# The last gathered slot on its own, the second block buffer cleared by DMA, and new instruction orders in a one-core recommendation tower

## The reference

```python
e = jnp.stack([tbl_0[ids[:, 0]], ..., tbl_49[ids[:, 49]]], axis=1)   # (512, 50, 16)
gram = jnp.einsum('bid,bjd->bij', e, e)
z = gram[:, _I_IDX, _J_IDX]                                          # the pairs i < j
h = jnp.concatenate([z, dense_ctx], axis=1)
h = jnp.maximum(h @ W_top1 + b_top1, 0.0)                            # 512
h = jnp.maximum(h @ W_top2 + b_top2, 0.0)                            # 256
y = h @ W_top3                                                       # 1
```

## Time and profile before

| | before |
|---|---|
| median of 3 runs | 134.31 us (133.75 to 134.50) |
| the profiled execution | 134.14 us, its span 132.3 us |
| TensorE, weight loads | busy 88%, 80% of the span |
| VectorE, ScalarE, GpSimd | busy 68%, 55%, 66% |
| granted TensorE clock, mean | 0.974 |
| read from HBM | 10.68 MB |

### The profile page before, as it was taken

One profiled execution on the slowest core, in us unless ns is written; L12 is line 12 of the kernel. 1 busy time (PEld: TensorE's weight loads), 2 busy tenths in 40 slices (PEclk: granted clock), 3 DMA queues, 4 the chain that ended last, 5 costly groups with the idle time before them and its releaser, 6 DMA issues.

```text
span 132.3 us, 3154 instructions
## 1 busy us (share of the span) xinstructions
PE 116.3 (88%) x1266; PEld 105.6 (80%) x1266; DVE 90.5 (68%) x162; ACT 73.1 (55%) x106; POOL 87.8 (66%) x96
## 2 busy tenths in 40 slices
PE   0199699739999999999989999999989999998990
PEld 0189486529996999999976999997789999898980
DVE  5947857997977789984875599965959635424211
ACT  7765999999699659964521934012930142222210
POOL 2777877877877778777777787787787787750000
PEclk9999999975699999999999999999999999999999
DMA  2999999993530100001011000000010000010000
GB/s 40 260 265 294 380 380 368 373 338 75 185 130 10 10 10 7 5 7 16 5 7 12 5 7 7 10 11 6 9 12 5 7 12 5 7 12 0 5 0 1
DMA packets 9411, 10.92 MB, mean 83 GB/s; under 512 B 2667, under 2 KB 6411, under 8 KB 9395
## 3 DMA queue, kind: packets, MB, share of 16 engines
q1 hardware_dynamic: 6453, 9.96, 22.8%
q0 software_dynamic: 2944, 0.76, 5.7%
HBM read 10.68 MB, written 0.03 MB: 81 GB/s over the span
## 4 chain that ended last, share of the span: by engine, by line
POOL 65%; issue 21%; PE 6%; DMA 3%; DVE 2%; POOLq 1%; DVEq 0%
POOL moving L317 33%; POOL moving L312 32%; DMA moving<-tbl,ids_sb 2%; PE psm L886 2%; PE gram L879 2%; DMA ids_sb<-in_ids 1%; PE pt L949 1%; POOLq L104 1%; DVE blocks L222 1%; PE p L886 1%; PE gram L886 1%; DVE mcols L659 0%; DVE h2w L704 0%; DVEq L667 0%; DVEq L653 0%
## 5 line engine op out<-in xcount | busy, mean ns | idle before, releaser
L317 POOL DMA_INDIRECT moving<-tbl,ids_sb x48 | 45.6, 950 | 14.6 <-issue 14.6
L312 POOL DMA_INDIRECT moving<-tbl,ids_sb x44 | 41.9, 953 | 15.5 <-issue 13.1
L886 PE MATMUL p<-z,w_sb 128*128 128x128 f32 x312 | 38.7, 275 | 0.0
L834 PE MATMUL psm<-table,onehot 128*128 128x160 f32 (+1 forms) x208 | 34.6, 317 | 3.9 <-DVE picked L588 3.3
L886 PEld LDWEIGHTS p<-z,w_sb 128*128 128x128 f32 x312 | 37.0, 192 | 0.8 <-issue 0.4
L834 PEld LDWEIGHTS psm<-table,onehot 128*128 128x128 f32 x208 | 30.6, 208 | 6.2 <-DVE picked L588 4.5
L577 DVE TENSOR_REDUCE fixed<-picked 128x48 f32<-128x480 f32 (+2 forms) x32 | 19.7, 635 | 0.2
L237 DVE COPY z<-gram 63x384 f32<-63x384 f32 (+1 forms) x18 | 9.3, 516 | 10.9 <-PE gram L879 6.8
L588 DVE TENSOR_TENSOR picked<-psm,mask_more 128x480 f32<-128x480 f32 x20 | 13.0, 651 | 5.0 <-PE psm L834 4.8
L222 ACT COPY blocks<-mcols 32x384 f32<-32x384 f32 (+3 forms) x15 | 13.0, 863 | 3.7 <-DVE mcols L659 3.5
L237 ACT COPY z<-gram 63x384 f32<-63x384 f32 (+1 forms) x18 | 7.8, 434 | 12.6 <-PE gram L879 10.0
(11 more groups left out here) (58 smaller groups left out, 102.7 us busy)
## 6 DMA issues: line engine op xcount, KB each, us to landing
w_sb<-in_w SPq DMA_DIRECT2D x12, 256.0 KB
wide<-quotients SPq DMA_DIRECT2D x9, 320.0 KB, 6.6
moving<-tbl,ids_sb POOLq DMA_INDIRECT x92, 2.4
table<-in_small SPq DMA_DIRECT2D x5, 240.0 KB, 3.6
table_big<-in_big SPq DMA_DIRECT2D x4, 200.0 KB
table<-in_small SPq DMA_DIRECT2D x2, 256.0 KB, 4.9
w_sb<-in_w SPq DMA_DIRECT2D x1, 512.0 KB, 10.0
table<-in_small SPq DMA_DIRECT2D x1, 192.0 KB, 5.1
```

The costliest lines, as they stand in the source:

```text
L312: nc.gpsimd.indirect_dma_start(moving[:, t, YS + n, 0:D], None, tables[n - 1], bass.IndirectOffsetOnAxis(ap=large_ids[:, t, n:n + 1], axis=0),
L317: nc.gpsimd.indirect_dma_start(moving[:, t, XS + n, 0:D], None, tables[HALF + n - 1], bass.IndirectOffsetOnAxis(ap=large_ids[:, t, HALF + ...
L834: ins = nc.tensor.matmul(psm[:, m % 2, START[f] - START[a]:START[f + 1] - START[a]], onehot[:, t % 2, f, :], table[:, START[f]:START[f + 1 ...
L886: return nc.tensor.matmul(hidden_sums(t, k), w1_sb[:, c, P * k:P * (k + 1)], z[:, t % 2, c, :], start=first, stop=last)
```

## The change

It has three parts. The tail of tile 3 is cut once more: slots 7 to 11 keep `tail_gathered`, slot 12 has a semaphore of its own, and VectorE turns and copies the five slots first and slot 12 behind them; ScalarE raises and copies the five and then copies slot 12. `product_x(3, CUT, YS)` is as before and waits for both pieces. Half 1 of `blocks` is cleared by 8 DMAs that SyncE issues behind W3's and ahead of the wait for `load_wide(3)`; each reads 1,600 bytes of zeros from DRAM into each of the 128 partitions. ScalarE's `clear(blocks[:, 1])` goes. Half 0 is cleared as before. The call lists of PE, ACT and DVE have a new order; on TensorE `second_layer(0)` now stands ahead of `product_y(1)`, `product_x(2)` ahead of all chunks of layer 2, and both selections 6 and 7 of tile 1 ahead of `product_x(0)`.

```diff
@@ -61,6 +61,8 @@
+CLEARS = 8
@@ -92,7 +94,7 @@
-def build_tower(nc, quotients, ids, ids_t, extra, small, big, w1, w2, b2, w3, consts_in, ident_in, out, *tables):
+def build_tower(nc, quotients, ids, ids_t, extra, small, big, w1, w2, b2, w3, consts_in, ident_in, zeros_in, out, *tables):
@@ -163,6 +165,7 @@
+        last_gathered = sem("last_gathered")
@@ -187,7 +190,8 @@
-        zeroed = [sem(f"zeroed{n}") for n in range(2)]
+        zeroed = sem("zeroed")
+        emptied = sem("emptied")
@@ -220,6 +224,10 @@
+        def piece(a):
+            return (a >= CUT) + (a == YS - 1)
@@ -290,6 +298,9 @@
+            for n in range(CLEARS):
+                part = blocks[:, 1, QP // CLEARS * n:QP // CLEARS * (n + 1)].rearrange("p j s q -> p (j s q)")
+                sp.dma_start(part, zeros_in.to_broadcast([P, QP // CLEARS * MS * Q])).then_inc(emptied, 16)
@@ -314,10 +325,13 @@
+                    landed = late_gathered[t]
+                    if t == TILES - 1 and XS + n >= CUT:
+                        landed = tail_gathered if XS + n < YS - 1 else last_gathered
                     nc.gpsimd.indirect_dma_start(
                         moving[:, t, XS + n, 0:D], None, tables[HALF + n - 1],
                         bass.IndirectOffsetOnAxis(ap=large_ids[:, t, HALF + n:HALF + n + 1], axis=0),
-                    ).then_inc(tail_gathered if t == TILES - 1 and XS + n >= CUT else late_gathered[t], 16)
+                    ).then_inc(landed, 16)
@@ -334,7 +348,7 @@
-            clear(blocks[:, 0, QP // 2:]).then_inc(zeroed[0], 1)
+            clear(blocks[:, 0, QP // 2:]).then_inc(zeroed, 1)
@@ -387,7 +401,10 @@
-                act.wait_ge(zeroed[t % 2], 2 - t % 2)
+                if t % 2:
+                    act.wait_ge(emptied, 16 * CLEARS)
+                else:
+                    act.wait_ge(zeroed, 2)
@@ -402,16 +419,19 @@
-                act.wait_ge(late_cols, t + (2 if a else 1))
+                act.wait_ge(late_cols, t + 1 + piece(a))
                 if t >= 2:
                     act.wait_ge(x_made, 2 * (t - 1))
-                act.wait_ge(zeroed[t % 2], 2 - t % 2)
+                if t % 2:
+                    act.wait_ge(emptied, 16 * CLEARS)
+                else:
+                    act.wait_ge(zeroed, 2)
...
-                act.wait_ge(late_cols, t + (2 if a else 1))
+                act.wait_ge(late_cols, t + 1 + piece(a))
@@ -459,55 +479,55 @@
-            onehots(1, 1)
             place_lower(0)
             shift(0)
-            clear(blocks[:, 1]).then_inc(zeroed[1], 1)
+            onehots(1, 1)
             raise_mid(0)
             spread_mid(0)
             onehots(1, 2)
+            raise_late(0, 0, YS)
             spread_late(0, 0, YS)
-            raise_late(0, 0, YS)
             unload_y(0)
             onehots(2, 0)
             onehots(2, 1)
+            onehots(2, 2)
             unload_x(0, 0, CH)
+            shift(1)
+            bias_part(0)
             place_lower(1)
-            bias_part(0)
-            shift(1)
+            bias_part(1)
+            onehots(3, 0)
+            bias_part(2)
             raise_mid(1)
-            onehots(2, 2)
-            onehots(3, 0)
             spread_mid(1)
+            hidden(0)
             onehots(3, 1)
-            bias_part(1)
-            bias_part(2)
-            hidden(0)
             unload_y(1)
+            spread_late(1, 0, YS)
             raise_late(1, 0, YS)
-            spread_late(1, 0, YS)
             unload_x(1, 0, CH)
+            shift(2)
             place_lower(2)
+            raise_mid(2)
+            spread_mid(2)
             onehots(3, 2)
-            raise_mid(2)
-            shift(2)
-            spread_mid(2)
             hidden(1)
             raise_late(2, 0, YS)
+            spread_late(2, 0, YS)
             unload_y(2)
-            spread_late(2, 0, YS)
+            unload_x(2, 0, CH)
+            shift(3)
             place_lower(3)
-            shift(3)
-            unload_x(2, 0, CH)
...
+            raise_late(3, 0, CUT)
             spread_late(3, 0, CUT)
-            raise_late(3, 0, CUT)
             unload_x(3, 0, CH - TAIL)
-            raise_late(3, CUT, YS)
-            spread_late(3, CUT, YS)
+            raise_late(3, CUT, YS - 1)
+            spread_late(3, CUT, YS - 1)
+            spread_late(3, YS - 1, YS)
@@ -527,7 +547,7 @@
-            nc.vector.memset(blocks[:, 0, 0:QP // 2], 0.0).then_inc(zeroed[0], 1)
+            nc.vector.memset(blocks[:, 0, 0:QP // 2], 0.0).then_inc(zeroed, 1)
@@ -639,7 +659,10 @@
-                dve.wait_ge(zeroed[t % 2], 2 - t % 2)
+                if t % 2:
+                    dve.wait_ge(emptied, 16 * CLEARS)
+                else:
+                    dve.wait_ge(zeroed, 2)
@@ -649,7 +672,9 @@
-                if a:
+                if a == YS - 1:
+                    dve.wait_ge(last_gathered, 16)
+                elif a:
@@ -661,8 +686,11 @@
-                dve.wait_ge(zeroed[t % 2], 2 - t % 2)
-                dve.wait_ge(late_cols, t + (2 if a else 1))
+                if t % 2:
+                    dve.wait_ge(emptied, 16 * CLEARS)
+                else:
+                    dve.wait_ge(zeroed, 2)
+                dve.wait_ge(late_cols, t + 1 + piece(a))
@@ -706,12 +734,18 @@
-            picks(0, 1, 3)
-            folds(0, 1, 3)
-            picks(0, 3, 5)
-            folds(0, 3, 5)
-            picks(0, 5, NSC)
-            folds(0, 5, NSC)
+            pick(0, 1)
+            fold(0, 1)
+            picks(0, 2, 4)
+            fold(0, 2)
+            pick(0, 4)
+            fold(0, 3)
+            pick(0, 5)
+            fold(0, 4)
+            pick(0, 6)
+            fold(0, 5)
+            pick(0, 7)
+            folds(0, 6, NSC)
@@ -720,75 +754,71 @@
+            spread_mid(0)
+            pick(1, 3)
             fold(1, 1)
-            pick(1, 3)
-            spread_mid(0)
             turn_late(0, 0, YS)
-            pick(1, 4)
             fold(1, 2)
+            picks(1, 4, 6)
             spread_late(0, 0, YS)
-            pick(1, 5)
             fold(1, 3)
             pick(1, 6)
-            fold(1, 4)
+            folds(1, 4, 6)
+            unload_y(0)
             pick(1, 7)
-            fold(1, 5)
-            unload_y(0)
-            fold(1, 6)
+            folds(1, 6, NSC)
             pick_big(1)
-            fold(1, 7)
+            unload_x(0, 0, CH)
             fold_big(1)
-            pick(2, 0)
+            picks(2, 0, 2)
+            bias_less(0)
+            fold(2, 0)
+            bias_less(1)
             turn_mid(1)
-            pick(2, 1)
-            bias_less(0)
             pick(2, 2)
-            unload_x(0, 0, CH)
-            fold(2, 0)
+            spread_mid(1)
+            fold(2, 1)
+            turn_smalls(1)
             pick(2, 3)
-            spread_mid(1)
-            turn_smalls(1)
-            fold(2, 1)
+            folds(2, 2, 4)
             pick(2, 4)
-            fold(2, 2)
-            pick(2, 5)
-            bias_less(1)
-            fold(2, 3)
+            last_layer(0)
             unload_y(1)
             turn_late(1, 0, YS)
+            fold(2, 4)
+            pick(2, 5)
+            spread_late(1, 0, YS)
             pick(2, 6)
-            fold(2, 4)
-            spread_late(1, 0, YS)
-            folds(2, 5, 7)
+            fold(2, 5)
             pick(2, 7)
+            fold(2, 6)
...
-            picks(3, 0, 3)
-            fold(3, 0)
+            picks(3, 0, 2)
+            folds(3, 0, 2)
             turn_mid(2)
-            fold(3, 1)
+            pick(3, 2)
+            fold(3, 2)
             pick(3, 3)
-            folds(3, 2, 4)
+            turn_smalls(2)
             pick(3, 4)
-            turn_smalls(2)
-            pick(3, 5)
             spread_mid(2)
-            folds(3, 4, 6)
-            last_layer(0)
-            pick(3, 6)
+            folds(3, 3, 5)
+            picks(3, 5, 7)
             turn_late(2, 0, YS)
+            spread_late(2, 0, YS)
+            fold(3, 5)
+            pick(3, 7)
             fold(3, 6)
             unload_y(2)
-            pick(3, 7)
+            pick_big(3)
             fold(3, 7)
-            spread_late(2, 0, YS)
-            pick_big(3)
-            fold_big(3)
             unload_x(2, 0, CH)
             dve.wait_ge(x_made, 4)
             nc.vector.memset(scols[:, 1, :, LATE + CUT - XS:], 0.0).then_inc(cleared, 1)
+            fold_big(3)
@@ -798,8 +828,10 @@
-            turn_late(3, CUT, YS)
-            spread_late(3, CUT, YS)
+            turn_late(3, CUT, YS - 1)
+            spread_late(3, CUT, YS - 1)
+            turn_late(3, YS - 1, YS)
+            spread_late(3, YS - 1, YS)
@@ -869,7 +901,7 @@
-                    pe.wait_ge(late_blocks[half], spread_by(half, t, 2 if a else 1))
+                    pe.wait_ge(late_blocks[half], spread_by(half, t, 3 if a else 1))
@@ -963,57 +995,59 @@
-            selections(0, 1, 3)
+            select(0, 1)
             broadcast(3)
-            select(0, 3)
+            select(0, 2)
```

(51 more changed lines are left out.)

## The result

The changed kernel takes 141.99 us (median of 6 runs), the kernel before 134.07 in the same series; the ratio of comparable runs is 1.055 (95% interval 1.051 to 1.058). It is 5% slower; 134.4 us was forecast, with 136.2 as the upper end. The profiled execution takes 140.74 us, span 138.8, against 134.14 and 132.3 before. Two of its six runs, at 143.17 and 203.5 us, were slow ones and stay out of the ratio, as do the ten experiments that ran where the kernel before itself took 239 to 257 us.

What follows compares the result with a forecast made beforehand. GpSimd's row of gathers was taken as the bound, TensorE almost as late. Tail -0.45, ScalarE's clear 0, delayed gather after absorption +0.53: +0.08 on 134.14, 134.22 us, so a median of 134.4, range 133.5 to 136.2 (8 in 10).

Steps and rivals of the forecast that it cites:

- the backlog at 366 GB/s: DMA queue at 28.7 us: clears make the backlog 2.2 MB, 6.1 us at that rate, engines busy to 34.8.
- T: Start of turn_late(0), after tile 0's last late gather lands: between 33.3 and 36.6 us, taken as 35.1.
- pieces of 1,600 bytes are smaller: Gather behind the clears: landing taken as 4.6 us, below the loaded rows, as wide loads have 2,560 bytes.
- first_layer(0) starts at T + 9.25: TensorE in the tile after turn_late(0): 44.35 us at T = 35.1, 1.6 us late against 42.75.
- T + 4.5: Start of product_x(0) after VectorE's transpose, fold, picks and copies, with selections 6 and 7 fitting in beside it.
- What the later waits absorb: TensorE up to product_y(3): two waits, 1.07 us together, shrink the 1.6 us of lateness to 0.53.
- the 0.33 us behind it: TensorE's wait at product_x(3, 0, CUT): no help, since last_layer(2) precedes turn_late(3, 0, CUT) and waits for TensorE.
- The tail: End of tile 3: only slot 12 left after the last gather, 0.45 us saved, at most 0.55.
- ScalarE's clear: ScalarE at 25.25 us: dropping its 2.85 us copy saves 0, as nobody on the chain waited for it.
- The orders: From product_x(1) on: the same matmuls in another order, TensorE's sum up to product_y(3) unchanged, 0.
- Rival B: Gather under load: T at 36.2 or above, 135.5 us, or 137.5 with TensorE's lower clock; chance 0.27 for both.
- The rule weighed from the Trainium skill: Gather beside the clears: waits one packet, 1.2 us, landing 4.0, T = 34.5, time 133.9 us.

Runs made afterwards that it cites:

- e7: The changed kernel with ScalarE's clear back in place of the DMAs of zeros, extra input kept: 132.83 us, ratio 0.991 to the kernel before.
- e16: The changed kernel with ScalarE's clear and without the extra DRAM input, so new orders and tail alone: 133.96 us, ratio 0.998 to the kernel before.
- e14: The kernel before with only the second cut of the tail: 134.36 us against 134.53, ratio 0.998.
- e13: The kernel before with only the 8 DMAs of zeros from one row in place of ScalarE's clear: 141.56 us, ratio 1.053.
- e15: The kernel before with one more DRAM input of 1,600 bytes that nothing reads: 133.46 us, ratio 0.993.
- e12: The changed kernel with each partition reading its own 1,600-byte row of zeros, still eight DMAs: 134.07 us, ratio 0.998 to the kernel before.
- e17: The changed kernel with one DMA of zeros instead of 8, one row of 12,800 bytes for all partitions: 137.91 us, ratio 1.027 to the kernel before.

## Why the prediction was wrong, step by step

**The step that failed: the backlog at 366 GB/s.** The prediction took 2.2 MB at the rate of the earlier trace rows, 6.1 us, and the engines idle by 34.8 us. From one short row the rate is 116 to 118 GB/s, at which the 1.64 MB alone take some 14 us. From there came T: "between 33.3 and 36.6" was reckoned from landings beside a queue at full speed. Measured: 42.4. With a source that keeps the queue at full speed T is 36.0, inside that range, and the time 134.07, where 134.4 was forecast. That the two times agree is luck in part: at T = 36.0 the prediction's own sum gives 134.31 - 0.45 + 2.5 - 1.07 = 135.3, and the measured time has the 0.8 us of the store in it, which nobody had forecast. The mechanism was right (the gather behind the clears, pick 4 behind turn_late(0), selection 6 behind pick 4), and the rate of the transfer was assumed rather than bounded: the reading that "pieces of 1,600 bytes are smaller" and so kinder asked for their size and not for their source; the 2,560-byte loads that it compared them with were broadcasts too, at 366 GB/s. A bound from below was nowhere in the range.

**T and what follows it.** "first_layer(0) starts at T + 9.25": measured T + 9.7 (42.42 to 52.14, and 36.01 to 45.68 with own rows). Selections 6 and 7 were to fit in beside the copies, with product_x(0) at T + 4.5. VectorE's copies were done in time, at 46.12 (T + 3.7), but TensorE had stood idle for 7.04 us and was granted 0.50 from 42 to 47 us, the lower of its two levels: the 14 matmuls took 3.35 us, where the chain shows 16 such matmuls in 1.98 at 71.27, and product_x(0) started at 47.71, T + 5.3. The 0.8 us shrink to 0.5 because product_x(0) and select_big(1) took 4.43 us together where 4.75 was forecast.

**What the later waits absorb.** 1.07 us by product_y(3) was forecast; measured 9.4 - 8.2 = 1.2. That the 0.33 us behind it do not help was wrong: between the two products that the earlier trace rows show at 107.39 and 114.38 another 0.4 us went (8.2 to 7.8), and the wait at the tail's product took a further 0.4 (7.8 to 7.3). Before, turn_late(3, 0, CUT) sat idle for 0.21 us behind last_layer(2) (112.05); in the changed kernel it follows at once, at 119.93. So last_layer(2), by which the prediction tied that transpose to TensorE, was not what it waited for last.

**The tail.** 0.45 us forecast: 0.4 in the profiles of e7 and e16, where TensorE is in time, about 0.2 in the timed pair of e14. In the changed kernel it gives nothing, since TensorE arrives at 128.9 and all slots had landed by then.

**ScalarE's clear.** Forecast 0; e7, which has it back, starts product_y(3) at 107.41 and the tail's product at 121.13, at the gathers' pace, so it costs nothing there. **The orders.** Forecast 0 at usual speed; measured none beyond the tail (e16 against e14, both 0.998), within some 0.3 us.

**Rival B** had the right side, mechanism and point of decision, but its price ended at T = 36.2. The clock's part in it was real: for product_x(0) about 1.2 us by an estimate from the copies' end at 46.12 and its usual 0.35 behind them, less than the 2 us that it was given. The rule weighed from the Trainium skill ("DMA: Bandwidth & Descriptors", queues, rings and completion order), that a DMA engine drains one packet of a queue before it turns to the next, was made into an estimate of T = 34.5. With own rows T was 36.0, a landing of 5.3 us where the estimate had 4.0: one packet a turn, counted once, is too little. Whether the engines take turns that way no run here shows.

**Not foreseen:** the 0.8 us of the store. The changed kernel has them too, so the clears cost it some 8.2 us, by an estimate, and not the 7.4 that the ratio shows; e13, the clears alone, gives the same beside e15 (1.053 / 0.993 = 1.060, 8 us).

## What to carry to other kernels

Before a broadcast or fill from DRAM is costed at the queue's best rate, ask how many bytes are distinct: a short row (here 1,600 bytes) read by every partition may run at a third of it, and every small transfer on the same engines is slowed with it. Cost a bulk load not by who waits for it but by who shares its engines: here nobody waited for the clears, and one 64-byte-a-row gather issued behind them cost 8 us. And the version that beats both kernels keeps ScalarE's clear, 2.85 us of an engine that nothing on the chain waits for there; most of its gain, 0.8 to 0.9 of 1.3 us, is the extra input's, and 0.2 to 0.4 the tail's.

When a change adds or removes a DRAM tensor, compare the landing of the last store in both profiles before the difference is credited to anything else.

## What the runs showed of the hardware

- One row of 1,600 bytes read for 128 partitions: 116 to 118 GB/s, engines 43% to 47% busy. The same volume from 128 rows: 329 to 350. From one row of 12,800 bytes, in one DMA: 341. From rows of 2,560 bytes (load_wide in the kernel before): 366. Which part of the memory sets this wasn't tried.
- A gather's landing: 2.4 us beside an idle queue, 5.3 beside pieces of 1,600 bytes at full rate (issued at 30.66, 36.0 in e12), 7.4 beside pieces of 12,800 bytes (issued at 30.80, 38.2 in e17), 11.9 beside the slow broadcast (12.8 in e13).
- The store of 2 KB of results lands in 1.4 us with one more input of 1,600 bytes in the program, or of 204,800 (own rows, e12), and in 2.2 to 2.6 us without; with an input of 12,800 bytes (e17) in 2.3. That the place of y_out in DRAM is the cause fits all of these, but was only argued: the place itself wasn't varied alone.
